# Reordering the opening of a one-core transformer layer: loads, projections and stores of the first batch, and nine constant products ahead of them

## The reference, cut to what matters

```python
x = layernorm(x + self_attention(x, Wq, Wk, Wv))        # x: 2 x 1024 x 256, 16 heads of 16
x = layernorm(x + cross_attention(x, ctx, mask, ...))   # ctx: 2 x 77 x 256
x = layernorm(x + mixture_of_8_experts_top_2(x, ...))
# self_attention: q, k, v = x @ Wq.T, x @ Wk.T, x @ Wv.T; softmax(q k.T / 4) v, no mask
```

## Time and profile before

| | us |
|---|---|
| median of 3 runs | 852.78 |
| lowest and highest | 852.44, 854.45 |
| profiled execution | 856.25 |
| its span | 854.4 |
| PE busy, DVE busy, ACT busy, POOL busy | 713.2, 639.0, 487.8, 305.5 |
| chain that ended last: PE, DVE, DMA | 54%, 26%, 6% |

### The profile page before, as it was taken

One profiled execution on the slowest core, in us unless ns is written; L12 is line 12 of the kernel. 1 busy time (PEld: TensorE's weight loads), 2 busy tenths in 40 slices (PEclk: granted clock), 3 DMA queues, 4 the chain that ended last, 5 costly groups with the idle time before them and its releaser, 6 DMA issues.

```text
span 854.4 us, 14878 instructions
## 1 busy us (share of the span) xinstructions
PE 713.2 (83%) x4760; PEld 332.1 (39%) x4760; DVE 639.0 (75%) x1087; ACT 487.8 (57%) x982; POOL 305.5 (36%) x249
## 2 busy tenths in 40 slices
PE   6789999999999999999998868867679888789800
PEld 3442222223222222222222235545367566667600
DVE  3487888877888888887875689999737446689765
ACT  2225677777777677776777554342436566457622
POOL 8000600000000398881002575666712554444411
PEclk9898999999999999999999888887679999899965
DMA  7746040030400689883000090000241333412121
GB/s 196 187 110 148 16 93 21 19 75 20 94 20 25 155 239 278 260 253 125 2 1 1 1 380 14 1 2 7 75 124 52 100 105 90 143 53 90 58 99 49
DMA packets 51171, 80.75 MB, mean 95 GB/s; under 512 B 16468, under 2 KB 35415, under 8 KB 49689
## 3 DMA queue, kind: packets, MB, share of 16 engines
q1 hardware_dynamic: 37065, 44.91, 19.2%
q0 software_dynamic: 9952, 31.29, 11.8%
q10 hardware_dynamic: 4080, 3.61, 1.7%
HBM read 48.21 MB, written 33.11 MB: 95 GB/s over the span
## 4 chain that ended last, share of the span: by engine, by line
PE 54%; DVE 26%; DMA 6%; issue 5%; ACT 4%; POOL 2%; SPq 1%; DVEq 1%; another core or an unknown queue 1%; ACTq 0%; POOLq 0%
PE bank L544 12%; PE bank L536 12%; PE quad L517 11%; DVE rowmax L959 6%; PE quad L868 6%; PE bank L885 5%; DMA kstack<-k_parts 3%; PE bank L468 2%; DVE hl L1189 2%; DVE sc L1062 2%; ACT probs L1495 2%; DVE sum L1074 2%; DVE max L1069 2%; DMA qstack<-q_parts 1%; DVE attn_all L1175 1%
## 5 line engine op out<-in xcount | busy, mean ns | idle before, releaser
L959 DVE TENSOR_REDUCE rowmax<-quad 128x1 f32<-128x1024 f32 x256 | 303.0, 1218 | 77.1 <-PE quad L517 76.5
L1495 ACT ACTIVATE probs<-bank 128x512 f32<-128x512 f32 x512 | 284.3, 595 | 115.6 <-PE bank L536 112.8
L536 PE MATMUL bank<-qstack,kstack 98*128 98x512 bf16 x512 | 195.0, 389 | 12.9 <-ACT probs L1495 11.2
L517 PE MATMUL quad<-kstack,qstack 96*128 96x512 bf16 x512 | 178.4, 388 | 15.2 <-DVE rowmax L959 6.6
L868 PE MATMUL quad<-xbT,w 128*128 128x128 bf16 x1104 | 121.1, 224 | 25.6 <-DVE hl L1189 16.0
L544 PE MATMUL bank<-probs,v_all 128*32 128x512 f32 x1024 | 140.3, 617 | 0.0
L536 PEld LDWEIGHTS bank<-qstack,kstack 98*128 98x128 bf16 x512 | 49.0, 97 | 193.9 <-ACT probs L1495 163.2
L868 PEld LDWEIGHTS quad<-xbT,w 128*128 x1104 | 91.3, 100 | 58.5 <-issue 43.3
L1619 ACT ACTIVATE hid<-quad,b 128x128 f32<-128x128 f32 x184 | 52.6, 369 | 65.1 <-PE quad L868 49.5
L517 PEld LDWEIGHTS quad<-kstack,qstack 96*128 96x128 bf16 x512 | 48.6, 99 | 77.4 <-DVE rowmax L959 39.8
L1839 POOL DMA_INDIRECT y_tokens<-ysb,dest x46 | 47.7, 1038 | 84.1 <-DVE ysb L1203 75.3
(11 more groups left out here) (184 smaller groups left out, 951.3 us busy)
## 6 DMA issues: line engine op xcount, KB each, us to landing
xb<-x_sorted SPq DMA_DIRECT2D x46, 129.0 KB
x_sorted<-blank POOLq DMA_DIRECT2D x6, 774.0 KB, 9.1
w1raw<-in_w POOLq DMA_DIRECT2D x8, 512.0 KB, 6.1
w2raw<-in_w POOLq DMA_DIRECT2D x8, 512.0 KB, 6.3
w_split<-w1two POOLq DMA_DIRECT2D x8, 512.0 KB, 5.7
w_split<-w2two POOLq DMA_DIRECT2D x8, 512.0 KB, 4.4
w<-w_split SPq DMA_DIRECT2D x16, 256.0 KB, 5.2
w<-w_split SPq DMA_DIRECT2D x4, 1024.0 KB, 11.8
```

The lines of the kernel that those rows point to most:

```text
L517: mm = pe.matmul(bank[2 * (p % 2) + e], q, kstack[slot][0:MAXROW, j, e * 512:e * 512 + 512], start=True, stop=True)
L536: mm = pe.matmul(bank[4 + i % 2], kstack[slot][0:KROWS, j, kt * P:kt * P + P], qstack[slot][0:KROWS, half, j, :], start=True, stop=True)
L959: dve.tensor_reduce(rowmax[:, k % 2, p:p + 1], quad[:, 2 * (p % 2):2 * (p % 2) + 2, :].rearrange("p a n -> p (a n)"), AX_X, ALU.max).then_ ...
L1495: act.activation(probs[:, i % PR, :], bank[4 + i % 2], ACT.Exp, scale=INV4).then_inc(probs_ready, 1)
```

## The change

- x's first two groups are loaded first, from two queues: SP issues wq, x 0, wv, the identity; ACT issues wk, x 1. Nine of ACT's 14 early loads go to the end of `load_late` on SP (6 loads become 15); the five that stay (`cwk`, `cwv`, `ctxT`, `cbk`, `cbv`) are issued by ACT after its fourth high part.
- x 2 and x 3 are issued by SP after the first stack has landed, and not before it.
- POOL sets `ones16` first; PE multiplies it with itself nine times, 512 columns each, into bank 3, with no use of the result.
- The eight jobs run in a row, each with its own bank; the four `project_v` come behind them and wait for `rest` of job 6 and job 7, whose banks they take over.
- The parts have five buffers, not four. ACT issues the store of its own high part for jobs 0 to 3; SP issues the other two.
- ACT makes high 4 to 7, waits for the stores, issues its three `kstack` loads, and then copies v 0 to 3.
- `efull` and `upto` move to DVE's work after the row maxima of unit 15, beside its wait for the late loads.

```diff
-SOON = 14
-LATE = 6
+SOON = 5
+LATE = 15
-RING = 4
+RING, PARTS, WARM = 4, 5, 9
...
-        QK_BANK = [(4, 5, 0, 1)[n % 4] if n < EARLY_JOBS else 7 for n in range(QK_JOBS)]
+        QK_BANK = [(4, 5, 0, 1, 2, 3, 6, 7)[n] if n < EARLY_JOBS else 7 for n in range(QK_JOBS)]
...
+            load_weight(sp, 0)
+            load_input(sp, 0)
+            load_weight(sp, 2)
+            sp.dma_start(ident[:, :], t["ident"]).then_inc(loaded["const_loaded"], 16)
...
+                late += [(block8[:, :], t["block8"]), (iota[:, :], t["iota"]), (slots[:, :], t["slots"]),
+                         (cbq[:, :], t["cbq"].rearrange("(h p) -> p h", p=P)), (wg[:, :, :], t["wg"].rearrange("(c p) n -> p c n", p=P)),
+                         (bg[:, :], t["bg"].rearrange("(o n) -> o n", o=1).to_broadcast([P, NE]))]
+                late += [(rows[n][:, :], t[n].rearrange("(o n) -> o n", o=1).to_broadcast([P, D])) for n in ("cbo", "gamma", "beta")]
...
             def store_parts(n):
-                for part in range(3):
+                if n >= RING:
+                    sp.wait_ge(parts_stored[n % RING], 48 * (n // RING))
+                for part in range(0 if n >= 4 else 1, 3):
...
             load_group(0, 0)
-            load_input(2)
-            load_input(3)
             sp.wait_ge(stack_loaded[0], 16 * LOADS)
+            load_input(sp, 2)
+            load_input(sp, 3)
...
-                    elif 4 <= n < EARLY_JOBS:
-                        pe.wait_ge(rest_done, n - 3)
...
+                    if m < 2:
+                        pe.wait_ge(rest_done, EARLY_JOBS - 1 + m)
...
-            for n in range(4):
+            pe.wait_ge(warm_set, 1)
+            for k in range(WARM):
+                pe.matmul(bank[3], ones16[:, :], ones16[:, :].rearrange("p (o q) -> p o q", o=1).to_broadcast([P, 4, P]), start=True, stop=True)
+            for n in range(EARLY_JOBS):
                 for c in range(C2):
                     project(n, c)
             for m in range(4):
-                for c in range(C2):
-                    project(4 + m, c)
                 project_v(m, range(4))
...
+            load_weight(act, 1)
+            load_input(act, 1)
             act.wait_ge(v_zeroed, 2)
             act.activation(credit[:, 6:7], v_all[:, 0, 0, 0, HD:HD + 1], ACT.Exp)
             for n in range(4):
                 high(n)
+                act.wait_ge(hi_done, n + 1)
+                store_part(act, n, 0)
+            with nc.allow_non_contiguous_dma(reason="small bias vectors go over the partitions"):
+                for dst, src in soon:
+                    act.dma_start(dst, src).then_inc(loaded["soon_loaded"], 16)
+            for n in range(4, EARLY_JOBS):
+                high(n)
+            for i in range(RING):
+                act.wait_ge(parts_stored[i], 48)
+            for row, part, n in K_BLOCKS:
+                src = scratch["k"][0:1, part:part + n, :, :].rearrange("o r d (g s) -> g (o r d) s", g=2)[0]
+                act.dma_start(kstack[0][row:row + n * HD, :, :].rearrange("p j s -> p (j s)"), src).then_inc(stack_loaded[0], 16)
             for m in range(4):
-                high(4 + m)
                 keep_values(m)
...
+            pool.memset(ones16[:, :], 1.0).then_inc(warm_set, 1)
+            pool.wait_ge(warm_set, 1)
             pool.memset(v_all[:, :, :, :, HD:HD + 1], 1.0).then_inc(v_zeroed, 1)
```

More of the change, by code:

```diff
@@ L166, in build @@
         qstack1, kstack1 = sb1("qstack1", [P, 2, GH, 512], BF16), sb1("kstack1", [P, GH, S], BF16)
-        parts = sb1("parts", [P, RING, 3, 512], BF16)
+        parts = sb1("parts", [P, PARTS, 3, 512], BF16)
         rest = sb1("rest", [P, 2, 512])
@@ L301, in unit_slot, with store_part, load_input, load_weight @@
             return (k // 2) % 2
+        def store_part(eng, n, part):
+            g, w, half = JOBS[n]
+            b, name = g // 2, "qk"[w]
+            layout = {"q": "d (h j s) -> h j d s", "k": "d (j h s) -> h j d s"}[name]
+            kept = part if name == "q" else 2 - part
+            dst = scratch[name][b * 2 + half, kept, :, :].rearrange(layout, h=2, s=512)[g % 2]
+            eng.dma_start(dst, parts[:, n % PARTS, part, :]).then_inc(parts_stored[n % RING], 16)
+        def load_input(eng, g):
+            eng.dma_start(xT[:, :, g * 512:(g + 1) * 512],
+                          t["xT"].rearrange("(c p) n -> p c n", p=P)[:, :, g * 512:(g + 1) * 512]).then_inc(xT_loaded[g], 16)
+        def load_weight(eng, i):
+            n = ("wq", "wk", "wv")[i]
+            eng.dma_start(w_in[n][:, :, :], t[n + "T"].rearrange("(c p) n -> p c n", p=P)).then_inc(w_loaded[i], 16)
         def await_outputs(eng, h):
@@ L353, in store_parts @@
                         sp.wait_ge(parts_done, n - 3)
-                    kept = part if name == "q" else 2 - part
-                    dst = scratch[name][b * 2 + half, kept, :, :].rearrange(layout, h=2, s=512)[g % 2]
-                    sp.dma_start(dst, parts[:, n % RING, part, :]).then_inc(parts_stored[n % RING], 16)
+                    store_part(sp, n, part)
             def load_group(pair, slot):
@@ L703, in rank @@
                 if g == 0:
[L704 removed]
+                    pe.wait_ge(constants_done, 1)
                 for i in range(4):
@@ L943, in _ @@
                     split_low(n)
[L944 to L955, removed]
             def reduce_max(u, k, p):
@@ L1445, in high @@
                 act.wait_ge(qk_ready, n + 1)
-                if n >= RING:
-                    act.wait_ge(parts_stored[n % RING], 48 * (n // RING))
-                act.activation(parts[:, n % RING, 0, :], bank[QK_BANK[n]], ACT.Copy).then_inc(hi_done, 1)
+                if n >= PARTS:
+                    act.wait_ge(parts_stored[(n - PARTS) % RING], 48 * ((n - PARTS) // RING + 1))
+                act.activation(parts[:, n % PARTS, 0, :], bank[QK_BANK[n]], ACT.Copy).then_inc(hi_done, 1)
             def keep_values(m):
@@ L1460, in _ @@
             soon = [(w_in[n][:, :, :], t[n].rearrange("(c p) n -> p c n", p=P)) for n in ("cwk", "cwv")]
[L1461 to L1466, removed]
+            soon += [(ctxT[:, :, :], t["ctxT"].rearrange("(c p) n -> p c n", p=P)), (cbk[:, :], t["cbk"].rearrange("(h p) -> p h", p=P)),
+                     (rows["cbv"][:, :], t["cbv"].rearrange("(o n) -> o n", o=1).to_broadcast([P, D]))]
             assert len(soon) == SOON
-            with nc.allow_non_contiguous_dma(reason="small bias vectors go over the partitions"):
-                for dst, src in soon:
-                    act.dma_start(dst, src).then_inc(loaded["soon_loaded"], 16)
+            load_weight(act, 1)
+            load_input(act, 1)
             act.wait_ge(v_zeroed, 2)
@@ L1698, in _ @@
                 pool.wait_ge(mid_done, n + 1)
-                pool.tensor_tensor(parts[:, n % RING, 2, :], rest[:, n % 2, :], parts[:, n % RING, 1, :], ALU.subtract).then_inc(low_done, 1)
+                pool.tensor_tensor(parts[:, n % PARTS, 2, :], rest[:, n % 2, :], parts[:, n % PARTS, 1, :], ALU.subtract).then_inc(low_done, 1)
             count = [0]
@@ L1710, in _ @@
             step(pool.memset(vbd[:, :, :, :, :], 0.0))
-            pool.memset(ones16[:, :], 1.0).then_inc(constants_done, 1)
             pool.memset(credit[:, 5:6], 0.0).then_inc(v2_zeroed, 1)
```

31 lines of the change are left out of this document (8 added, 23 removed).

## The result

The changed kernel takes 859.16 us (median of 20 runs, 856.60 to 861.93) beside 854.54 us for the kernel before on the same chip (20 runs, 852.44 to 858.94): ratio 1.0046, 95% interval 1.0032 to 1.0060. It is slower by 0.46%, 3.9 us; 3.1 us faster was forecast. The profiled execution has a span of 857.3 us.

What follows compares the result with a forecast made beforehand. The bound was when the first stack lands and how fast the row maxima then run. Terms -0.8 (kstack issue) - 0.8 (x behind stack) - 1.5 (row maxima) = -3.1 us: median 852.78 to 849.7, range 847.0 to 852.6.

Steps and rivals of the forecast that it cites:

- x first, and the products: Opening: x 0 lands at 7.3 us, no gain; nine constant products give back 0 of 2.4 us of slow clock.
- rival A: First jobs: constant products carry the clock over; first row maximum 2.5 us earlier, total 848.8 us; chance 0.20.
- The low parts: POOL, jobs 0 to 3: fourth low part ends at 19.7 to 20.0 us, last store issued at 19.8 to 20.1.
- The landing of the last store: Before the kstack loads: lands in 3.5 us, not 4.13; ACT's five early loads could take that 0.6 back.
- the 24.25 of the sum: ACT's kstack loads issued at 24.25 us, right behind high 7, not at 25.04: gain 0.8 us.
- x 2 and x 3 behind the stack: First stack load: without x beside it 0.8 us shorter; bounds 0 and 2.8.
- the sign of being wrong that I had named: First stack load: the prediction is wrong if the stack takes 11 us without x beside it.
- v behind the jobs: v 0 to 3: rest 6 done at 24.4 to 26 us, last v at 31.3 to 33, before the stack; no cost.
- rival B: First row maximum: clock down again after a gap without work, only 1.6 us gain stays, total 851.2; chance 0.20.
- The row maxima: Row maxima of unit 0: clock stays up, gain 1.5 us; bounds 0 and 1.8.
- Late loads: SP before unit 1's negative maxima: nine more issues cost 5 us, hidden in 7.6 us.
- Rival C: Unit 1: SP's late issues are slow and hold it; up to 14 us slower, 867; chance 0.06.

Runs made afterwards that it cites:

- f4: The changed kernel without the nine constant products; ratio 1.0057 to the kernel before.
- h2: h1 with 16 constant products for nine; ratio 0.9985 to the kernel before, 845.98 beside 848.08 us.
- f1: The changed kernel with ACT's five loads issued right behind wk and x 1, not behind high 3; ratio 1.0037 to the kernel before, 850.88 us.
- g3: f3 with x 2 and x 3 issued by SP before its wait for the stack; ratio 0.9989 to the kernel before.
- f2: The changed kernel with the nine added late loads issued behind unit 1's negative maxima; ratio 1.0037 to the kernel before, 851.60 us.
- g2: f3 with POOL taking the low parts of jobs 0 to 3 ahead of its fills; ratio 1.0024 to the kernel before.
- h3: f3 with only cwk, cwv, ctxT issued first, cbk and cbv still behind high 3; one execution, kstack loads issued at 24.6 us.
- g1: The kernel before, unchanged, profiled a second time; first row maximum at 37.5 us, unit 2 at 116.5.
- h4: f1 with only the three broadcast rows (cbo, gamma, beta) behind unit 1's negative maxima; one execution, no ratio, unit 0 takes 28.5 us.
- g4: The kernel before with nine of ACT's opening loads moved to the end of the late ones, and the two constants; ratio 1.0051 to the kernel before.
- f3: The changed kernel with the edits of f1 and f2 together; ratio 1.0001 to the kernel before, median 847.41 beside 848.21 us.
- h1: f3 with the second kstack fill behind DVE's work on jobs 4 to 7 and kstack loads ahead of high 7; ratio 0.9997 to the kernel before.

## Why the prediction was wrong, step by step

- **x first, and the products: right.** x 0 landed at 7.49 (7.3 foretold), with the DMA engines at a share of 0.97. By the rule of the Trainium skill, page "DMA: Bandwidth & Descriptors", section "Issuing engines are not separate DMA queues", a second queue only saves issue time; the trace agrees (349 GB/s from 5 to 8 us, x 0 0.4 us later than before). The products' share was put at 0 and f4 shows 0 at the first row maximum. Of the two reasons given only the gap held: after 3.8 us of products, less than the 4.7 of the rows, the clock did rise. That a longer run of them carries over (h2) speaks for rival A's mechanism; here the gap of 2.6 us undid it.
- **The low parts: right.** The fourth ended at 19.90 (19.7 to 20.0), the last store was issued at 20.24 (19.8 to 20.1): the gain of the issue was 0.6 us.
- **The landing of the last store: the first step that failed.** I named the five loads and let them "take that 0.6 back". They took 3.3: the term that was put at 3.5 us measured 6.78, and the wait for the store, not high 7, set the `kstack` issue. The bound came from the trace of before, where nothing but the stores themselves was moving from 20 to 25 us; a price for stores beside 0.8 MB of loads stood in no row, and its upper bound should have been at least the time of that traffic (0.8 MB at the 162 to 349 GB/s of the opening's stretches above: 2.3 to 4.9 us). With the five loads gone (f1) the landing is 3.92 and the `kstack` issue 23.92, against the 24.25 of the sum.
- **x 2 and x 3 behind the stack: the size failed.** 0.8 foretold, 0 found (g3), with 0.4 not ruled out. It was the lower bound that I had named, and the sign of being wrong that I had named came true: the stack took 11.8 us without x beside it.
- **v behind the jobs: half right.** `rest` 6 was done at 27.2, not at 24.4 to 26, as ACT's five issues took 4.6 us and held high 4 until 22.3. The last v ended at 36.8, still ahead of the stack, and the clock fell in the gap as rival B had it.
- **The row maxima: near in size, by luck.** 1.5 foretold, 1.3 found, but the 1.5 stood on a clock that stays up, and it was at 0.50 here too until 42.3: 3.4 us of it, where it had been 6.2. With the clock up the row maxima take 23.0 us (f2, g2, h3), which would have been 2.3 less than before and over my bound of 1.8; the clock took 1.0 of that back. Beside g1 only 0.3 are found.
- **Late loads: the second step that failed.** I priced their issues on SP (5 us; they took 7.0, in 7.6 of room) and put their transfers, which stand ahead of the negative maxima in the same queue, at nothing without a reason. Rival C had the right place, SP's late loads and unit 1, at a chance of 0.06, but its mechanism, the issues, was not the one that acted. Nor does a full queue explain its long issues: only `block`, right behind xres, took 2.53 us, and `iota` behind it 0.54, with xres in flight until 88.2. Its room, too, was read off wrongly: the first score of unit 1 was at 90.63, not at 91.28, 3.8 us after the maxima were there. The landing took 5.2 and not 1.7. PE waited 1.86 us, which made unit 0 1.5 us longer than in the first profile of the kernel before, and the clock behind the wait cost unit 1 another 1.6.

Added up: forecast -0.8 - 0.8 - 1.5 = -3.1. Found at unit 2: +2.5 (first row maximum), -1.3, +1.5, +1.6, together +4.2 when the unrounded starts are taken, beside 3.9 us in the total.

## What to carry to other kernels

A load that is moved out of the way goes somewhere: list every transfer that will then be in flight, or ahead in the same queue, when the next one on the critical path is issued, and price it by its bytes and its form, not only by its issue. When a stage's opening is held by the landing of its last store, nothing large belongs into the microseconds before that. A run of dummy products was worth something here only when it reached nearly to the real work: 1.06 us short of it kept the clock, 2.6 us short lost it. And before a gain is put down to a change, look how long the clock was low in that stretch of both profiles: over the row maxima the time went with it, from 23.0 to 25.5 us, between kernels that do the same work there.

## What the runs showed of the hardware

- A DRAM row broadcast to 128 partitions was a slow transfer: three of 128 KB moved at 62 GB/s with the DMA engines at 0.68 (changed kernel, 89 to 92 us) and at 87 GB/s with them at 0.35 (h4, 88 to 91 us), where the 1 KB packets of xres had gone at 340 to 380 GB/s.
- A store of 128 KB on the way to the stack landed 3.7 to 4.2 us after its issue with nothing but stores in flight (before, g1, g4, f1, f3, h1, h2), and 6.7 to 7.0 us after it beside 0.8 MB of loads (changed, f2, f4).
- A DVE cast from float32 to bfloat16 took 0.43 us alone and 3.79 or 2.37 beside a POOL fill of `kstack` (g2).
- The granted clock rose at 4.8 us, after 3.8 us of constant products, and was taken back at 8.2 after 2.6 us without work (changed kernel); with 1.06 us without work it stayed (h2). The Trainium skill, page "TensorE: Matmul & The Clock Gate", section "What's actually happening", says that activity releases the throttle; the trace agrees: products of ones raised the clock.
- The stack's six loads (1.57 MB) took 11.4 to 12.1 us from issue to use, with 1 MB of x beside them (before, g1, g3, g4: 11.4 to 12.1) or without (11.4 to 11.8).
